# Attention: row maxima over two score banks per reduction, values of two key blocks multiplied in one visit, a DVE transpose in place of TensorE's

## The reference

```
q = heads(x @ Wq);  k_s, v_s = heads(x @ Wkv_short);  k_l, v_l = heads(x @ Wkv_long)
decay_bias = -|pos_k - pos_q| * (1 - decay_factor)
out_short = softmax(q k_s^T / sqrt(32) + decay_bias) v_s
out_long  = softmax(q k_l^T / sqrt(32)) v_l
out = (alpha * out_short + (1 - alpha) * out_long) @ Wo      # alpha = sigmoid(mix_weight)
```

## Time and profile before

| | us |
|---|---|
| median of 3 runs (4902.56 to 4904.38) | 4903.04 |
| span of the profiled execution | 4900.3 |
| attention, about 490 to 3790 | 3300 |
| TensorE busy in the span | 4717.9 |
| DVE busy | 4038.9 |
| POOL busy | 3278.9 |
| ACT busy | 2978.9 |

### The profile page before, as it was taken

The page is one execution under the profiler, slowest core; times in us unless marked ns, Lnnn a source line. Parts: engine busy times, 40 slices in busy tenths (PEclk is TensorE's granted clock), DMA queues, the critical chain, the costliest instruction groups (busy, mean ns, idle before and its releaser), DMA issues. The chain is left out here.

```text
span 4900.3 us, 100056 instructions
## 1 busy us (share of the span) xinstructions
PE 4717.9 (96%) x30796; PEld 2078.4 (42%) x30796; DVE 4038.9 (82%) x6609; ACT 2978.9 (61%) x5170; POOL 3278.9 (67%) x1267
## 2 busy tenths in 40 slices
PE   8998999999999999999999999999998699999998
PEld 3444333333333333333333333333332477777776
DVE  7567888888888888888888888888884488888887
ACT  3222477777777767777777777767766355555554
POOL 0000498998989989898998989989898233333332
PEclk9999799999999999999999999999999799999999
DMA  5444366666666666666666676666755100000000
GB/s 171 126 140 130 92 149 153 152 154 158 147 156 151 152 157 147 160 146 158 152 153 157 145 160 152 152 153 145 165 134 114 67 27 21 27 27 27 27 23 12
DMA packets 207465, 592.51 MB, mean 121 GB/s; under 512 B 37043, under 2 KB 110899, under 8 KB 157941
## 3 DMA queue, kind: packets, MB, share of 16 engines
q0 software_dynamic: 55008, 400.58, 37.4%
q1 hardware_dynamic: 151919, 185.58, 12.6%
q10 hardware_dynamic: 38, 0.08, 0.0%
HBM read 123.56 MB, written 61.64 MB: 38 GB/s over the span
## 5 line engine op out<-in xcount | busy, mean ns | idle before, releaser
L877 DVE TENSOR_REDUCE rowmax_parts<-scores_qk 128x1 f32<-128x512 f32 x4096 | 2525.9, 681 | 427.0 <-PE scores_qk L954 426.8
L862 ACT ACTIVATE probs_T<-scores_kq 128x512 f32<-128x512 f32 x4096 | 2288.4, 597 | 955.4 <-PE scores_kq L954 857.7
L800 POOL TENSOR_TENSOR probs_added<-probs_added,probs_T 128x2048 f32<-128x2048 f32 x510 | 2387.0, 4680 | 49.5 <-POOL probs_added L800 35.7
L954 PE MATMUL scores_kq<-q_operand,k_operand 103*128 103x512 f16 (+3 forms) x3712 | 1274.6, 349 | 19.5 <-ACT probs_T L862 17.4
L954 PE MATMUL scores_qk<-k_operand,q_operand 96*128 96x512 f16 (+4 forms) x3712 | 1121.6, 351 | 42.4 <-DMA v_operand<-v_dram 15.0
L1025 PE MATMUL outputs_T<-probs_T,v_operand 128*32 128x512 f32 x8192 | 1092.7, 605 | 1.3 <-ACT probs_T L862 1.3
L954 PEld LDWEIGHTS scores_kq<-q_operand,k_operand 103*128 103x128 f16 x3712 | 358.4, 97 | 934.6 <-ACT probs_T L862 688.0
L954 PEld LDWEIGHTS scores_qk<-k_operand,q_operand 96*128 96x128 f16 (+1 forms) x3712 | 354.6, 98 | 432.0 <-DVE rowmax_parts L877 186.6
L1650 PE MATMUL f_gate_up<-w_gate_up,xq_T 128*128 128x256 f16 (+1 forms) x4608 | 494.3, 266 | 7.7 <-DVE hidden L1541 6.6
L812 POOL DMA_DIRECT2D probs_poured<-probs_T x318 | 276.7, 870 | 266.1 <-DMA probs_poured<-probs_T 192.8
L1650 PEld LDWEIGHTS f_gate_up<-w_gate_up,xq_T 128*128 128x128 f16 x4608 | 421.4, 99 | 76.8 <-issue 24.3
(11 more groups left out here) (167 smaller groups left out, 4134.8 us busy)
## 6 DMA issues: line engine op xcount, KB each, us to landing
probs_poured<-probs_T POOLq DMA_DIRECT2D x382, 1024.0 KB, 7.6
qk_parts_dram<-qk_parts SPq DMA_DIRECT2D x96, 256.0 KB, 2.8
q_operand<-qk_parts_dram SPq DMA_DIRECT2D x192, 128.0 KB, 2.6
k_operand<-qk_parts_dram SPq DMA_DIRECT2D x192, 128.0 KB, 4.0
v_dram<-v_heads SPq DMA_DIRECT2D x16, 1024.0 KB, 6.5
v_operand<-v_dram SPq DMA_DIRECT2D x64, 256.0 KB, 6.1
q_operand_above<-qk_parts_dram SPq DMA_DIRECT2D x96, 128.0 KB, 2.9
x_groups<-x SPq DMA_DIRECT2D x8, 1024.0 KB, 9.3
```

Source lines behind the costliest of these rows:

```text
L800: nc.gpsimd.tensor_tensor(total, first, probs[:, b % PBUF, :], ALU.add).then_inc(added.sem, 1)
L862: nc.scalar.activation(probs[:, kb % PBUF, qt * BANK:(qt + 1) * BANK], pb[:, k % 2, :], ACT.Exp)\
L877: nc.vector.reduce_max(rowmax[:, w % 2, c // NQ, c % NQ:c % NQ + 1], pa[:, k % 3, :], AX.X)\
L954: return nc.tensor.matmul(out, lhsT, rhs, start=start, stop=stop, skip_group_check=True)
```

## The change

The maxima get four PSUM banks in two pairs (the bank of the transposes goes to them): TensorE signals after every second chunk, and DVE reduces two banks, 1024 columns, with one instruction (`max_pair`), so that 32 parts are left for `negate`. `negate` writes f16, 16 of 32 columns of `negmax`, the others being zero. DVE transposes these 32 x 32 blocks itself (`turn_max`, behind the first pair of step 10), which leaves the maxima of a unit on four groups of 16 partitions; `place_max` therefore takes four DMAs for each operand row, of 16 runs of 64 bytes each: four for an odd unit, eight for an even one. TensorE's transpose and ACT's rounding are gone.

TensorE's order now runs over two steps at a time: `times_v` of blocks i and i+1, the `counts` of both steps, and then eight scores for exp and eight for maxima in turn, beginning with `scores(i + 2, 2)` and ending with a chunk of maxima of step i+1. Scores for exp stand up to one key block further ahead of `times_v` than before; ten of the first unit's are computed ahead of the loop instead of six. The two banks of `scores_kq` stay.

```diff
--- before.py
+++ after.py
@@ -581,6 +581,7 @@
 KB = L // P
 NQ = L // BANK
 CHUNKS = KB * NQ
+PAIRS = CHUNKS // 2
 UNITS = 4
 PASSES = B * NH // 2
 PBUF = 8
@@ -592,6 +593,7 @@
 ASTEPS = 10
 
 TURN_MAX = 10
+SQUARE = 32
 INVERT = 7
 WEIGH = 11
 MIX = 12
@@ -639,9 +641,9 @@
         probs = sb("probs_T", [P, PBUF, L], F32)
         added_sum = sb("probs_added", [P, 2, L], F32)
         poured_sum = sb("probs_poured", [P, 2, L], F32)
-        rowmax = sb("rowmax_parts", [P, 2, KB, NQ], F32)
-        negmax = sb("negmax", [P, 2, KB], F32)
-        maxT = sb("negmax_T", [KB, 2, P], F16)
+        rowmax = sb("rowmax_parts", [P, 2, KB, 2], F32)
+        negmax = sb("negmax", [P, 2, SQUARE], F16)
+        maxT = sb("negmax_T", [P, 2, SQUARE], F16)
 
         oT = sb("o_T", [P, 2, BANK], F32)
         o_w = sb("o_weighed", [P, BANK], F32)
@@ -649,24 +651,23 @@
         ident = sb("ident_f32", [P, P], F32)
         ident16 = sb("ident_f16", [P, P], F16)
 
-        pa = ps("scores_qk", [P, 3, BANK], F32)
+        pa = ps("scores_qk", [P, 4, BANK], F32)
         pb = ps("scores_kq", [P, 2, BANK], F32)
         po = ps("outputs_T", [P, BANK], F32)
         pc = ps("sums", [P, BANK], F32)
-        pt = ps("turned", [P, BANK], F32)
 
         consts = sem("a_consts")
         chain = sem("a_const_chain")
+        cleared = sem("a_negmax_cleared")
         rows = [sem(f"a_rows{i}") for i in range(2)]
         zeroed = sem("a_zeroed")
         v_written = PENDING["v stored"]
         passed = sem("a_passed")
         opened = [Rises(sem(f"a_opened{w}"), 10 - 3 * (w % 2), 16) for w in range(UNITS)]
-        maxrow = [Rises(sem(f"a_maxrow{w}"), 2 - w % 2, 16) for w in range(UNITS)]
-        scoredA = Rises(sem("a_scored_qk"), UNITS * CHUNKS)
-        maxed = Rises(sem("a_maxed"), UNITS * (CHUNKS + 1), credit=1)
+        maxrow = [Rises(sem(f"a_maxrow{w}"), 4 * (2 - w % 2), 16) for w in range(UNITS)]
+        scoredA = Rises(sem("a_scored_qk"), UNITS * PAIRS)
+        maxed = Rises(sem("a_maxed"), UNITS * (PAIRS + 1), credit=1)
         turned = Rises(sem("a_max_turned"), UNITS)
-        roundm = Rises(sem("a_max_rounded"), UNITS)
         scoredB = Rises(sem("a_scored_kq"), UNITS * CHUNKS)
         expd = Rises(sem("a_exp"), UNITS * CHUNKS, credit=1)
         summed = Rises(sem("a_pv"), UNITS * KB, credit=1)
@@ -727,9 +728,11 @@
 
             def place_max(w, n):
 
-                sp.wait_ge(roundm.sem, roundm.at(n, w + 1))
+                sp.wait_ge(turned.sem, turned.at(n, w + 1))
                 for dst in (q_op[w], q_up[w]) if w % 2 == 0 else (q_op[w],):
-                    sp.dma_start(dst[MROW:MROW + 1, :], maxT[:, w % 2, :]).then_inc(maxrow[w].sem, 16)
+                    row = dst[MROW:MROW + 1, :].rearrange("o (t b c) -> o t b c", t=KB, c=SQUARE)
+                    for b in range(P // SQUARE):
+                        sp.dma_start(row[:, :, b, :], maxT[b * SQUARE:b * SQUARE + KB, w % 2, :]).then_inc(maxrow[w].sem, 16)
 
             def store(p, n):
 
@@ -775,6 +778,7 @@
         def _(pool):
             give_credit(pool, [maxed, expd, summed, added, counted, taken, weighed, counted_poured] + stored)
             nc.gpsimd.memset(ones[:, :], 1.0).then_inc(consts, 1)
+            nc.gpsimd.memset(negmax[:, :, :], 0.0).then_inc(cleared, 1)
             nc.gpsimd.memset(ident[:, :], 0.0).then_inc(chain, 1)
             pool.wait_ge(chain, 1)
             nc.gpsimd.affine_select(out=ident[:, :], in_=ident[:, :], compare_op=ALU.not_equal, fill=1.0, base=0,
@@ -829,25 +833,11 @@
 
         @block.scalar
         def _(act):
-            def round_max(w, n):
-                act.wait_ge(turned.sem, turned.at(n, w + 1))
-
-                if w >= 2:
-                    act.wait_ge(maxrow[w - 2].sem, maxrow[w - 2].at(n, maxrow[w - 2].per_pass))
-                elif not isinstance(n, int) or n > 0:
-                    s = maxrow[w + 2]
-                    act.wait_ge(s.sem, s.before(n, s.per_pass))
-                nc.scalar.copy(maxT[:, w % 2, :], pt[0:KB, 0:P]).then_inc(roundm.sem, 1)
-
             load_positions(act, 0)
-            round_max(0, 0)
 
             def one_pass(n, first, last):
                 for w in range(UNITS):
                     for kb in range(KB):
-
-                        if kb == (TURN_MAX + 2) % KB and after(w, n, last):
-                            round_max(*after(w, n, last))
 
                         u, b = divmod(w * KB + kb - PBUF, KB)
                         act.wait_ge(summed.sem, summed.at(n, u * KB + b + 1))
@@ -871,22 +861,33 @@
         @block.vector
         def _(dve):
 
-            def max_chunk(w, n, c):
-                k = w * CHUNKS + c
+            def max_pair(w, n, g):
+                k = w * PAIRS + g
                 dve.wait_ge(scoredA.sem, scoredA.at(n, k + 1))
-                nc.vector.reduce_max(rowmax[:, w % 2, c // NQ, c % NQ:c % NQ + 1], pa[:, k % 3, :], AX.X)\
+                half = pa[:, 2 * (k % 2):2 * (k % 2) + 2, :].rearrange("p b q -> p (b q)")
+                nc.vector.reduce_max(rowmax[:, w % 2, g // 2, g % 2:g % 2 + 1], half, AX.X).then_inc(maxed.sem, 1)
+
+            def negate(w, n):
+                dve.wait_ge(maxed.sem, maxed.at(n, (w + 1) * (PAIRS + 1) - 1))
+                nc.vector.tensor_reduce(negmax[:, w % 2, 0:KB], rowmax[:, w % 2, :, :], AX.X, ALU.max, negate=True)\
                     .then_inc(maxed.sem, 1)
 
-            def negate(w, n):
-                dve.wait_ge(maxed.sem, maxed.at(n, (w + 1) * (CHUNKS + 1) - 1))
-                nc.vector.tensor_reduce(negmax[:, w % 2, :], rowmax[:, w % 2, :, :], AX.X, ALU.max, negate=True)\
-                    .then_inc(maxed.sem, 1)
-
-            for c in range(CHUNKS):
-                max_chunk(0, 0, c)
+            def turn_max(w, n):
+                dve.wait_ge(maxed.sem, maxed.at(n, (w + 1) * (PAIRS + 1)))
+                if w >= 2:
+                    dve.wait_ge(maxrow[w - 2].sem, maxrow[w - 2].at(n, maxrow[w - 2].per_pass))
+                elif not isinstance(n, int) or n > 0:
+                    s = maxrow[w + 2]
+                    dve.wait_ge(s.sem, s.before(n, s.per_pass))
+                nc.vector.transpose(maxT[:, w % 2, :], negmax[:, w % 2, :]).then_inc(turned.sem, 1)
+
+            for g in range(PAIRS):
+                max_pair(0, 0, g)
+            dve.wait_ge(cleared, 1)
             negate(0, 0)
-            for c in range(EARLY):
-                max_chunk(1, 0, c)
+            turn_max(0, 0)
+            for g in range(EARLY // 2):
+                max_pair(1, 0, g)
 
             def take(w, n):
 
@@ -928,10 +929,14 @@
                             weigh(*back)
                         distance, chunks = chunks_of(i)
                         unit = after(w, n, last, distance)
-                        for c in chunks if unit else ():
-                            max_chunk(*unit, c)
-                            if c == CHUNKS - 1:
+                        for c in chunks[::2] if unit else ():
+                            max_pair(*unit, c // 2)
+                            if c // 2 == PAIRS - 1:
                                 negate(*unit)
+                            if i == TURN_MAX and c == chunks[0]:
+                                turn_max(*ahead)
+                        if i == TURN_MAX and ahead and not unit:
+                            turn_max(*ahead)
                         if back and i == MIX and back[0] % 2:
                             mix(back[0] // 2, back[1])
 
@@ -966,16 +971,16 @@
             def scores_for_max(w, n, c):
 
                 t, kc = divmod(c, NQ)
-                k = w * CHUNKS + c
+                k = w * PAIRS + c // 2
                 if c == 0:
                     pe.wait_ge(opened[w].sem, opened[w].at(n, opened[w].per_pass))
 
-                if k >= 3:
-                    pe.wait_ge(maxed.sem, maxed.at(n, k - 2 + (k - 3) // CHUNKS))
-                else:
-                    m = max(j for j in range(UNITS * CHUNKS) if j % 3 == k)
-                    pe.wait_ge(maxed.sem, maxed.before(n, m + 1 + m // CHUNKS))
-                bank = pa[:, k % 3, :]
+                if c % 2 == 0 and k >= 2:
+                    pe.wait_ge(maxed.sem, maxed.at(n, k - 1 + (k - 2) // PAIRS))
+                elif c % 2 == 0:
+                    m = UNITS * PAIRS - 2 + k
+                    pe.wait_ge(maxed.sem, maxed.before(n, m + 1 + m // PAIRS))
+                bank = pa[:, 2 * (k % 2) + c % 2, :]
                 if w % 2:
                     last = score(bank, q_op[w][0:PARTS3, t * P:(t + 1) * P],
                                  k_op[w][0:PARTS3, kc * BANK:(kc + 1) * BANK], True, True)
@@ -987,13 +992,8 @@
                                      k_op[w][0:MROW, kc * BANK + r * P:kc * BANK + (r + m) * P], i == 0, side != 0)
                         if side == 0:
                             last = score(out, ident16[:, :], kinkA[:, :], False, True)
-                last.then_inc(scoredA.sem, 1)
-
```

(57 more changed lines are left out.)

## The result

The changed kernel takes 5069.13 us (5066.5 to 5079.15), the kernel before 4903.71 beside it: ratio 1.0336, 95% interval 1.0324 to 1.0348. It is slower by 3.4%. The profiled execution has a span of 5077.3 us.

What follows compares the result with a forecast made beforehand. Bound: TensorE's stream and one turn of the two-bank exp relay plus the visit, nearly meeting. Odd unit +2.4 us, even +1.35, 32 x 3.75 = 120, plus 3: 123 on 4900.3, 5023; median 5026, range 4935 to 5130.

Steps and rivals of the forecast that it cites:

- The hand-over in a round: Exp scores through two PSUM banks, three turns in a row: two merged steps +0.29 us (odd unit), +0.30 (even), five rounds each.
- s8: Last of the eight scores for exp in a round of two steps, put at 3.74 us after the first.
- late row: Row of maxima landing after TensorE asks for it, round of steps 12 and 13: about 1.1 us in 32 units.
- The pairs: DVE reductions of 1024 instead of 512, 1.13 us each; three rounds with reciprocals together -0.15 us a unit.
- The feared wait for a free pair of banks: TensorE's maxima scores waiting for a whole pair to be reduced: the upper end, +0.7 us a unit.
- The turned maxima: DVE's own transpose of the maxima, once in a unit: 0.2 us, at most 44 us in all, at least nothing.
- The row's DMAs: Four or eight transfers on SP, 0.74 us an issue, landing 2.9 later: eight land at 10.8 us, needed at 9.6.
- rival (c): Row or pairs much later, 3.5 us in 32 units or +0.7 x 64: 5100 us or somewhat more; chance 0.15.
- POOL: POOL's chain of poured sums gains room and waits for ACT's exps, not ACT for it; counted as nothing.
- Busy share of TensorE: Sign expected in the profile after: TensorE's busy share, 989 of 1000 us before, falling below 0.97.
- Rival (a): TensorE sets the pace and merged visits pay: round about 5.6 us with a kink, total 4839 us; chance 0.10.
- (b): Exps every 0.49 us with scores always ready: a round of 5.94 us, total 4905 us; chance 0.07.

Runs made afterwards that it cites:

- The third bank: Changed kernel with single maxima in three banks, and three scores_kq banks for exp scores instead of two: 5066.94 us, 1.0324 of the kernel before.
- the one with the early transpose: Changed kernel with DVE's transpose of the maxima directly behind the negation, before the reciprocal and a pair: 5023.24 us, 1.0231 of the kernel before.
- the kernel with steps: Changed kernel with TensorE's order of before, one visit and one step at a time: 4903.88 us, 0.9993 of the kernel before.

## Why the prediction was right, and where it was off

The sign, the cause and the size of the main term held; 5069 lies in the range, 43 us above the number.

- *The hand-over in a round.* Right. s8 was put at 3.74 us after s1 and came at 3.78 (2021.69 to 2025.47); a round of an odd unit at 6.15, measured 6.17 to 6.23, and 6.36 in an even unit, measured 6.35 to 6.36. TensorE's weight loads for these scores wait for exps more often than before, 1259 times instead of 946. Without the late row, units grew by 1.21 and 1.39 us, where 1.30 and 1.35 stood: 83 us against 85. That the even unit comes so near is in part luck: its five rounds without reciprocals grew by 1.28 instead of 1.50, and the other three by 0.12 where -0.15 stood. The third bank shows the cause in the rounds that DVE doesn't hold: with it, 5.96 us, their surplus is gone in even units and all but 0.10 us in odd ones.
- *The pairs.* The instruction takes 1212 ns, and in a run one starts 1.14 us after the other (median); 1.13 a pair was the estimate. The three rounds with reciprocals, put at -0.15 us, came to +0.12 in even units and -0.17 in odd ones. The feared wait for a free pair of banks stayed away: TensorE's wait for DVE fell from 164.9 to 77.7 us (1000 to 3000 us).
- *The turned maxima.* 0.20 us, as estimated, beginning 2.42 us after s1 for 2.5.
- *The row's DMAs.* This term was mis-sized: 1.1 us in 32 units, 35 us in all; measured 80 us in 31 units in the profile, and 73 by the ratios with and without the large transfer (0.0149 x 4905). The step that failed is the price of the transfers, taken from stores and loads issued at another time, 0.74 us an issue, and from a landing of 2.9 us, taken as belonging to the transfers themselves. Both depend on what else is in flight: 0.62 us an issue and a landing of 1.7 without the 1 MB, 0.95 and 1.7 to 3.1 with it. In the median the two errors nearly cancelled, which is luck: 8.1 us from first issue to landing in the prediction, 8.5 measured; in single units it is up to 9.9. So the lateness was put down to eight issues, which alone are in time. The prediction had nothing else queued with them at that moment; POOL's DMA was not looked at beside SP's, though it was in the trace of before. The larger row was rival (c), whose 3.5 us an odd unit was too much; the time lies between it and the forecast.
- *What the pause costs on top.* It was counted as the wait alone. TensorE waits for the row 51.8 us in 29 units from 560 to 3740 us, 1.8 us each; the clock, which the sum had no term for, adds 22.6 in 11 of them (last section). Together that is 74.4 of the 74.7 us by which the row lengthens these units.
- *POOL.* Right: it waits for exps (4.8 before, 79.3 us after), not ACT for it.
- *Busy share of TensorE.* It was to fall below 0.97 and is 0.975: a score counts 0.39 us but the next can start after 0.22, so a short pause between scores is partly booked as busy. That sign was chosen badly.
- *Rival (a)*, TensorE's pace, and *(b)*, the hand-over overlapping better: both refuted by 1.08 between scores. With a third bank (b)'s round of 5.94 appears, measured 5.96. Whether the change as a whole would be fast with a third exp bank isn't shown: with four banks for the pairs, one for the outputs and one for the sums, a third exp bank would be the ninth, and it wasn't tried.

## What to carry to other kernels

Where a matmul and an ACT operation hand data through two PSUM banks, look up the turn of that pair in a stretch without other load and count how many turns stand between two pauses: merging the pauses saves less than the turns that then stand in a row cost. A step that is split into many small transfers is priced with the large transfers that are in flight at that moment, of any engine, beside it; the trace of before shows them. And an engine's gain can go to the next limit: with DVE relieved and steps kept, the steps at which ACT waits for POOL's landings grew by about what the steps with reciprocals had lost. That POOL's chain of landings was the limit there is read from the waits; the other order of POOL's work did not shorten its wait, so no run shows it.

## What the runs showed of the hardware that was not expected

Behind some of the pauses that the late row makes in an otherwise full TensorE, the granted clock falls to half, 1.2 of 2.4 GHz. Stretches of one such place (us; busy us of TensorE, weight loads, DVE, ACT, POOL; granted clock; DMA share; GB/s), and TensorE's rows in it:

```profile
1170.00:1176.40 6.40, 6.21 (x35) 1.70 (x33) 5.57 (x6) 4.45 (x9) 6.22 (x3) 1.00 0.85 167
1176.40:1179.77 3.37, 0.37 (x3) 0.01 (x1) 1.68 (x2) 0.78 (x2) 3.37 (x2) 0.77 0.29 86
1179.77:1185.25 5.48, 5.48 (x23) 1.34 (x24) 1.23 (x1) 1.19 (x2) 5.32 (x2) 0.52 1.01 233
1185.25:1190.00 4.75, 4.68 (x32) 1.85 (x32) 3.67 (x4) 4.09 (x8) 1.44 (x2) 1.00 0.57 141
```

```profile
1179.77 0.28 PE L959 MATMUL scores_kq<-q_operand,k_operand 103*128 103x128 f16 x1 [3.00 <-DMA q_operand_above<-negmax_T]
...
1181.80 3.52 PE L1025 MATMUL outputs_T<-probs_T,v_operand 128*32 128x512 f32 x16
1185.25 0.39 PE L959 MATMUL scores_kq<-q_operand,k_operand 103*128 103x512 f16 x1
```

After 3.00 us of waiting, a visit takes 3.45 us to the next score instead of 1.86 (2019.83 to 2021.69). From 560 to 3740 us the clock fell 11 times, for 51.2 us together, in the changed kernel, each time beside a wait for the row, of 1.36 to 3.00 us. The other 18 such waits, of 0.98 to 2.62 us, had no fall, so the length of the wait alone doesn't tell it. Two of the longest, one without a fall and one with:

```profile
2678.35 0.23 PE L959 MATMUL scores_kq<-q_operand,k_operand 103*128 103x128 f16 x1 [2.62 <-DMA q_operand_above<-negmax_T]
...
2679.44 1.92 PE L1025 MATMUL outputs_T<-probs_T,v_operand 128*32 128x512 f32 x16
2681.30 0.39 PE L959 MATMUL scores_kq<-q_operand,k_operand 103*128 103x512 f16 x1
```

```profile
2252.31 0.23 PE L959 MATMUL scores_kq<-q_operand,k_operand 103*128 103x128 f16 x1 [2.85 <-DMA q_operand_above<-negmax_T]
...
2253.40 3.61 PE L1025 MATMUL outputs_T<-probs_T,v_operand 128*32 128x512 f32 x16
2256.95 0.39 PE L959 MATMUL scores_kq<-q_operand,k_operand 103*128 103x512 f16 x1
```

The visit takes 1.86 us to the next score in the one and 3.55 in the other. This shows the clock's price apart from the wait's: in 17 of the 18 units without a fall the two rounds exceed 6.19 and 6.31 us by the wait and 0.01 us (0.17 in the first), in the 11 with a fall by 1.5 to 2.9 us more, 22.6 in all. The clock fell once, for 3.4 us, in the kernel before and in the one with the early transpose. The late row is not its only occasion: in the kernel with steps it fell 8 times, for 34.1 us, beside waits of TensorE for exps of 1.7 to 4.1 us, most of which ACT had begun late because of POOL's landings; so part of what the landings cost there is the clock.
